# Cross attention on one core: which engine makes the weight low parts, and the order of copies and exponentials in the first steps

## The reference

```
h = layernorm(x) * gamma + beta
Q = h @ Wq;  K = context @ Wk;  V = context @ Wv          # per head 64 wide
attn = softmax(Q @ K^T, axis=-1) * 64 ** -0.5
out = x + (attn @ V).reshape(256, 1024) @ Wo + bo
```

## Time and profile before

| | us |
|---|---|
| median of 3 runs | 364.79 (364.53 to 364.80) |
| the profiled execution: its own time | 364.5 |
| its span, from the first to the last instruction of the trace | 362.6 |
| TensorE matmul busy | 353.0 (97%) |
| ScalarE busy | 252.1 (70%) |
| VectorE busy | 242.9 (67%) |
| GpSimd busy | 164.5 (45%) |

### The profile page before, as it was taken

One profiled execution on the slowest core, in us unless ns is written; L12 is line 12 of the kernel. 1 busy time (PEld: TensorE's weight loads), 2 busy tenths in 40 slices (PEclk: granted clock), 3 DMA queues, 4 the chain that ended last, 5 costly groups with the idle time before them and its releaser, 6 DMA issues.

```text
span 362.6 us, 8915 instructions
## 1 busy us (share of the span) xinstructions
PE 353.0 (97%) x3116; PEld 305.8 (84%) x3116; DVE 242.9 (67%) x534; ACT 252.1 (70%) x762; POOL 164.5 (45%) x321
## 2 busy tenths in 40 slices
PE   5999999999999999999999999999999999999986
PEld 5779888888888888988888988888988888988865
DVE  5887566866568666686667675686565866566654
ACT  4898876766677766777766776766677766677762
POOL 5677884335444262444532464323744325344321
PEclk9999999999999999999999999999999999999999
DMA  6930010200002000020000100020000000000000
GB/s 191 272 118 3 1 52 2 82 0 3 2 0 82 0 0 0 0 80 0 1 0 29 51 0 0 0 78 1 0 0 0 29 2 0 2 2 31 3 0 31
DMA packets 10743, 10.39 MB, mean 29 GB/s; under 512 B 960, under 2 KB 10176, under 8 KB 10720
## 3 DMA queue, kind: packets, MB, share of 16 engines
q1 hardware_dynamic: 10192, 9.64, 8.6%
q10 hardware_dynamic: 416, 0.33, 0.3%
q0 software_dynamic: 112, 0.13, 0.2%
HBM read 8.00 MB, written 2.10 MB: 28 GB/s over the span
## 4 chain that ended last, share of the span: by engine, by line
PE 92%; ACT 3%; DVE 3%; DMA 1%; issue 0%; POOL 0%; DVEq 0%
PE mix_ps L710 16%; PE st_ps L805 15%; PE st_ps L688 13%; PE o_ps L777 12%; PE w_ps L752 12%; PE w_ps L730 12%; PE w_ps L823 10%; ACT prob L405 2%; DMA x_in<-in_x_dram 1%; PE w_ps L671 1%; PE w_ps L663 1%; ACT qk_hi L415 0%; DVE w_lo L480 0%; DVE neg_max L563 0%; DVE qk_lo L576 0%
## 5 line engine op out<-in xcount | busy, mean ns | idle before, releaser
L316 POOL TENSOR_SCALAR prob<-prob,inv 128x256 f32<-128x256 f32 x256 | 120.1, 485 | 158.0 <-DVE inv L570 157.6
L405 ACT ACTIVATE prob<-st_ps,neg_max 128x256 f32<-128x256 f32 x256 | 118.0, 473 | 27.0 <-DVE neg_max L563 27.0
L563 DVE TENSOR_REDUCE neg_max<-st_ps 128x2 f32<-128x512 f32 x128 | 82.5, 683 | 35.2 <-PE st_ps L688 34.9
L458 ACT ACTIVATE prob_t<-st_ps 128x512 f32<-128x512 f32 x64 | 38.4, 600 | 44.2 <-PE st_ps L805 44.2
L638 DVE COPY prob_t<-st_ps 128x512 f32<-128x512 f32 x64 | 44.1, 691 | 28.6 <-PE st_ps L805 25.2
L710 PE MATMUL mix_ps<-prob_t,v_sb 128*64 128x256 f32 x504 | 61.5, 385 | 0.1
L805 PE MATMUL st_ps<-ident,prob 128*128 128x128 f32 x512 | 61.1, 272 | 0.0
L805 PEld LDWEIGHTS st_ps<-ident,prob 128*128 128x128 f32 x512 | 56.7, 141 | 0.1
L576 DVE TENSOR_TENSOR qk_lo<-w_ps,qk_hi 128x512 fp32r<-128x512 f32 x62 | 42.8, 690 | 20.6 <-ACT qk_hi L415 20.6
L405 ACT ACTIVATION_READ_ACCUMULATOR prob<-st_ps,neg_max 128x1 f32 x256 | 52.7, 206 | 0.0
L710 PEld LDWEIGHTS mix_ps<-prob_t,v_sb 128*64 128x64 f32 x504 | 33.4, 136 | 17.9 <-issue 0.3
(11 more groups left out here) (121 smaller groups left out, 589.1 us busy)
## 6 DMA issues: line engine op xcount, KB each, us to landing
x_in<-in_x_dram SPq DMA_DIRECT2D x8, 256.0 KB, 3.1
out_dram<-y_sb SPq DMA_DIRECT2D x7, 256.0 KB, 2.2
c_in<-in_ctx_dram SPq DMA_DIRECT2D x7, 192.0 KB, 2.9
w_raw<-in_L_xattn_Wq_dram SPq DMA_DIRECT2D x8, 128.0 KB, 3.3
w_raw<-in_L_xattn_Wo_dram SPq DMA_DIRECT2D x4, 256.0 KB, 3.5
w_raw<-in_L_xattn_Wk_dram SPq DMA_DIRECT2D x4, 128.0 KB, 4.0
w_raw<-in_L_xattn_Wk_dram SPq DMA_DIRECT2D x8, 64.0 KB, 3.6
w_raw<-in_L_xattn_Wv_dram SPq DMA_DIRECT2D x2, 256.0 KB, 3.5
```

The lines of the kernel that those rows point to most:

```text
L316: last = nc.gpsimd.tensor_scalar(prob[:, e, r, :], prob[:, e, r, :], inv[:, e, r:r + 1], SCALE, ALU.mult, ALU.mult)
L405: last = nc.scalar.activation(prob[:, e, r, :], st_ps[e][:, r * ROWS:(r + 1) * ROWS], ACT.Exp, bias=neg_max[:, e, r:r + 1], accum_out=sums ...
L458: nc.scalar.activation(prob_t[:, e, :, :].rearrange("p a b -> p (a b)"), st_ps[e][:, :], ACT.Copy)\
L563: nc.vector.tensor_reduce(neg_max[:, e, :], st_ps[e][:, :].rearrange("p (r j) -> p r j", r=RT), AX, ALU.max, negate=True).then_inc(max_rea ...
```

## The change

Three low parts (4, 5, 8) go from VectorE to GpSimd and one (14) from GpSimd to VectorE. In step 0, VectorE scales the heads 1 and 3 itself (`scale`), with its own semaphore. On ScalarE, in step 0 the exponential of head 3 comes before `keys_hi(0)`, the high parts 11 to 13 go behind the copies, `context_hi(1)` moves from the head of step 1 to ahead of them; in step 1 the high part of 14 takes the place of 15, and 15 goes behind `keys_hi(1)`, ahead of 16. VectorE makes low part 9 between `maximum(1)` and `maximum(2)` of step 0, and does the statistics of sequence 1 and low part 13 behind the copies of step 0. GpSimd issues the load of `bo` later. TensorE's order is unchanged.

```diff
-    LO_VECTOR = (0, 4, 5, 8, 9, 13, 16)
-    LO_POOL = (1, 2, 3, 6, 7, 10, 11, 12, 14, 15, 17, 18, 19, 20, 21, 22, 23)
+    LO_VECTOR = (0, 9, 13, 14, 16)
+    LO_POOL = (1, 2, 3, 4, 5, 6, 7, 8, 10, 11, 12, 15, 17, 18, 19, 20, 21, 22, 23)
@@ GpSimd
-            for n in (1, 2, 3, 6, 7):
+            for n in (1, 2, 3, 4, 5, 6, 7, 8):
                 weight_lo(n)
-            pool.dma_start(bo_b[:, :], b_o.partition_broadcast(P)).then_inc(bo_in, 16)
@@ step
-                if u == 1:
-                    weight_lo(14)
...
-                    for e in range(HEADS):
+                    for e in (0, 2) if u == 0 else range(HEADS):
...
                         if e == 1 and u in (1, 2):
                             weight_lo({1: 15, 2: 21}[u])
+                if u == 0:
+                    pool.dma_start(bo_b[:, :], b_o.partition_broadcast(P)).then_inc(bo_in, 16)
@@ ScalarE
-                b = of_seq(u, SPLIT_C, 1)
+                b = of_seq(u, SPLIT_C, 2)
@@
-                if u == 1:
-                    weight_hi(14)
                 probabilities(0)
                 probabilities(1)
                 if u in (1, 2):
-                    weight_hi({1: 15, 2: 21}[u])
+                    weight_hi({1: 14, 2: 21}[u])
@@
                 probabilities(2)
+                if u == 0:
+                    probabilities(3)
                 keys_hi(0)
...
-                probabilities(3)
+                if u != 0:
+                    probabilities(3)
                 keys_hi(1)
...
                 if u == 0:
                     values_out(0, w0_ps)
-                    weight_hi(10)
-                    weight_hi(11)
                     values_out(1, w1_ps)
+                if u == 1:
+                    weight_hi(15)
                 if u == 1:
                     weight_hi(16)
@@
                         if u == 0 and e == 0:
-                            weight_hi(12)
-                            weight_hi(13)
+                            weight_hi(10)
+                if u == 0:
+                    act.wait_ge(c_turned, 2)
+                    context_hi(1, context_bank(1))
+                    for n in (11, 12, 13):
+                        weight_hi(n)
@@ VectorE
+                def scale(e):
+                    dve.wait_ge(inv_ready, e + 1)
+                    for r in range(RT):
+                        last = nc.vector.tensor_scalar(prob[:, e, r, :], prob[:, e, r, :],
+                                                       inv[:, e, r:r + 1], SCALE,
+                                                       ALU.mult, ALU.mult)
+                    last.then_inc(scaled_vector, 1)
                 maximum(0)
                 maximum(1)
+                if u == 0:
+                    weight_lo(9)
@@
                 inverse(1)
                 if u == 0:
-                    weight_lo(8)
-                    weight_lo(9)
+                    scale(1)
+                if u == 1:
+                    weight_lo(14)
@@
                 inverse(2)
-                if u == -1:
-                    weight_lo(4)
+                if u == 0:
+                    inverse(3)
+                    scale(3)
                 keys_lo(0)
-                if u == -1:
-                    weight_lo(5)
-                inverse(3)
+                if u != 0:
+                    inverse(3)
@@
                 keys_lo(1)
-                if u == 0:
-                    statistics(1, turns)
@@ behind and within the copies of heads 1 and 3
-                        if u == 0 and e == 1:
-                            weight_lo(13)
+                if u == 0:
+                    statistics(1, turns)
+                    weight_lo(13)
@@ TensorE, turn
-                    pe.wait_ge(scaled, HEADS * u + e + 1 + turns(32))
+                    if u == 0:
+                        pe.wait_ge((scaled, scaled_vector)[e % 2], e // 2 + 1)
+                    else:
+                        pe.wait_ge(scaled, HEADS * u + e - 1 + turns(32))
```

More of the change, by code:

```diff
@@ L154, in cross_attention_block @@
         scaled = sem("scaled")
+        scaled_vector = sem("scaled_vector")
         turned = sem("turned")
```

## The result

| | before | changed |
|---|---|---|
| median, us | 364.80 (6 runs, 364.53 to 364.82) | 367.81 (6 runs, 367.67 to 369.37) |
| profiled execution, its span | 364.5, 362.6 | 367.8, 365.9 |

By the medians the kernel is slower by 3.0 us (a ratio of 1.0083); 367.5 was forecast. The ratio over all runs is 1.0096 (95% interval 1.0076 to 1.0115). It is higher because two of the six runs, 369.13 and 369.37, are a group of their own, with a mean granted clock of 0.995 and 0.994 where the other four have 1.000.

What follows compares the result with a forecast made beforehand. TensorE, 92% of the chain, was taken as the bound. Head 3 of `turn(1)` starting 2.7 us later gave 364.5 + 2.7 = 367.2, as a median 367.5; this case alone 366.6 to 368.1, whole range 366.2 to 369.2.

Steps and rivals of the forecast that it cites:

- The mechanism: Step 1: GpSimd's in-order queue holds heads 2 and 3 behind low part 15, which waits for late high part 15; +2.7 us.
- second half of `scores(0)`: Step 0, TensorE: starts about 0.2 sooner than 13.54 without low part 5 ahead of `keys_lo(1)`.
- step 1's exponentials start: ScalarE, step 1: at 24.1 instead of 23.66, 0.4 later; bounds 0 or 0.9.
- high part 15 starts, is ready: ScalarE, step 1, behind `keys_hi(1)`: starts at 29.75, takes 0.65, ready at 30.4; before, it was made at 25.47.
- the port: Step 1: VectorE's low part 16 waits for GpSimd's low part 15, and head 2 for 16; 0.5, bounds 0 and 0.6.
- head 3's transposes: TensorE, `turn(1)`: head 3 starts at 34.1 instead of about 31.4, +2.7 us.
- TensorE's lead behind `scores(1)`: TensorE some 1.2 to 1.5 ahead after `scores(1)`, through three removed waits; used up in the wait at `turn(1)`.
- wait ahead of `output(0)`: TensorE, step 1: new wait of about 1.4; `mix_lo` comes at about 28.5, TensorE at 27.1.
- point 1: Start: low part 5 off VectorE ahead of `keys_lo(1)` starts second half of `scores(0)` about 0.2 sooner, at most 0.3.
- Rival A: TensorE's clock falls during its new idle time in step 1, costing 1.7 more: +4.4, 369.2; chance 0.31.
- Rivals B and C: B: faster, TensorE keeps its lead, 363.5, chance 0.03. C: no change, 364.8 to 365.2, chance 0.04.
- the late exponentials: Step 1, next late once low part 15 is out of the way: heads 2 and 3 scaled 0.4 to 0.5 behind before.

Runs made afterwards that it cites:

- e3: Kernel before, with only high part 15 moved behind `keys_hi(1)` of step 1 on ScalarE: 367.14 us, ratio 1.0073.
- e2: Changed kernel, with GpSimd's low part 15 moved behind head 3 of step 1, high part 15 still late: 365.25 us, ratio 1.0014.
- e6: Kernel of e2, with GpSimd holding low part 4 until VectorE has made both `h_lo`: 364.70 us, ratio 1.0000 to the kernel before.
- e7: Kernel of e6, with VectorE's low part 13 moved behind the second maximum of step 1: 363.96 us, ratio 0.9982 to the kernel before.
- e9: Kernel of e1, with VectorE's low part 16 held until GpSimd has scaled heads 2 and 3 of step 1: 365.65 us, ratio 1.0031.
- e8: Changed kernel, with VectorE's low part 16 held until GpSimd has scaled heads 2 and 3 of step 1: 367.36 us, ratio 1.0082.
- e4: Kernel before, with only low parts 4 and 5 moved from VectorE to GpSimd: 365.12 us, ratio 1.0014.
- e5: Kernel of e2, with low parts 4 and 5 back on VectorE: 364.80 us, ratio 1.0003 to the kernel before.
- e1: Changed kernel, with high part 15 moved back directly behind that of 14 on ScalarE: 366.35 us, ratio 1.0044 to the kernel before.

## Why the prediction was right, and where it was off

**The mechanism was the forecast's.** GpSimd's in-order queue held heads 2 and 3 behind a piece that ScalarE now makes last. e3 shows that this move is enough, e2 that its loss is taken back by the queue's order alone.

**The terms.**

| term | forecast | measured |
|---|---|---|
| second half of `scores(0)` | 13.3 | 14.18 |
| step 1's exponentials start | 24.1 | 24.73 |
| high part 15 starts, is ready | 29.75, 30.4 | 30.29, 31.0 |
| low part 15 | 1.28 | 1.27 |
| the port | 0.5 | 0.4 (2.29 less 1.90) |
| head 3's transposes | 34.1 | 34.66 |
| `values(0)` no longer waits | 0.44 gained | gone (17.10, next pass 17.80) |
| `scores(1)` starts | 21.0 | 21.68 |
| second half of `scores(1)` | no wait | at 22.49, no wait |
| TensorE's lead behind `scores(1)` | 1.2 to 1.5 | 0.80 (`mix(0)` at 23.29, 24.09 before) |
| wait ahead of `output(0)` | 1.4 | 0.91 |
| `scores(2)` starts | 36.2 | 36.84 |

From the exponentials on, every start is late by 0.54 to 0.64, and the lead of TensorE is short by 0.4 to 0.7. That is the one step that failed: under "what the change saves", point 1 took 0.2 as gained at the start. It was a loss, the second half of `scores(0)` being 0.64 later than before and 0.88 later than forecast. I had checked whether low parts 4 and 5 are ready in time on GpSimd, and not what they take from VectorE while they run. The rows that show it in the changed kernel:

```profile
9.80 0.43 DVE L532 TENSOR_TENSOR h_lo<-h_full,h_hi 128x256 fp32r<-128x256 f32 x1
10.15 0.95 DVE L535 TENSOR_TENSOR h_lo<-h_full,h_hi 128x256 fp32r<-128x256 f32 x1
```

GpSimd's low part 4 started at 9.88. Not all of the later start is the edit. TensorE worked at the lower clock for longer in this profile: the record of its granted clock in the trace begins at full speed 9.6 us into the span, and at 7.1 in the profile before (ahead of its first entry the views print 1.00), and four transposes of x took 1.12 at 7.26 where they took 0.66. This varies from run to run. The eleven profiles let the two be told apart by the start of the first half of `scores(0)`:

| full clock from | low part 4 not on GpSimd, or held (e6, e7) | low part 4 on GpSimd at once |
|---|---|---|
| 6.8 to 7.1 us | 12.26 (before), 12.25 (e6) | 12.78 (e9) |
| 7.8 to 8.0 us | none | 13.54 (e8), 13.57 (e4) |
| 8.9 to 9.7 us | 12.54 (e3), 12.52 (e5), 12.52 (e7) | 13.08 (changed), 13.06 (e1), 13.07 (e2) |

The late clock goes with 0.26 to 0.30 in either kind, low part 4 on GpSimd with 0.52 to 0.56 in the first and the last row; in the middle row it is more, since both `h_lo` are stretched there (0.90 and 0.94 in e8). By medians e5 and e6 put the price at 0.45 to 0.55. What point 1 did claim is true by itself: in e6, with the two low parts off VectorE and held back, the second half of `scores(0)` starts at 13.35, 0.19 sooner than before. The same exclusion was priced about rightly 20 us later, and was not looked for here.

That the median is off by only 0.3, less than the price of this step, is in part luck: with the start set right (e6) the exponentials of step 1 start at 23.90, 0.2 sooner than the 24.1 of the forecast, so two errors went against each other. TensorE's shorter lead mattered little, since it was to be used up in the wait at `turn(1)` and was. (The weights are 24 pieces, 0 to 23, and not 25; nothing here hangs on the count.)

**The port.** VectorE's low part 16 in the changed kernel:

```profile
31.54 1.35 DVE L486 TENSOR_TENSOR w_lo<-w_raw,w_hi 128x512 fp32r<-128x512 f32 x1
```

It took 1.35 and the multiplications 2.29 when both wanted to run, 0.69 and 1.85 when one was made to wait (e8). It started at 31.54, while low part 15 was running until 32.34, and ended at 32.89; the first multiplication, started at 32.31, took 0.92 and then ended at 33.23. The Trainium skill, "SBUF — State Buffer", section "SBUF: two separate sides", has the pair of ports locked by one of the two engines for a whole instruction while the other stands. These runs agree: VectorE lost 0.66, less than the 0.80 for which GpSimd's low part still ran, and GpSimd lost 0.44, less than the 0.69 of low part 16.

**Rival A happened too, in some of the runs.** In e8's profiled execution the clock fell. Its busy time by stretch (TensorE, weight load, VectorE, ScalarE, GpSimd, then granted clock):

```profile
32.00:34.00 2.00, 0.24 (x2) 0.24 (x3) 0.69 (x1) 0.44 (x1) 2.00 (x4) 1.00 0.00 0
34.00:36.00 2.00, 1.75 (x10) 1.37 (x9) 1.26 (x2) 1.55 (x5) 1.17 (x3) 0.78 0.00 0
36.00:38.00 2.00, 2.00 (x8) 1.53 (x6) 0.12 (x1) 0.70 (x2) 2.00 (x4) 0.50 0.03 8
38.00:40.00 2.00, 2.00 (x26) 1.58 (x24) 0.58 (x1) 1.18 (x3) 0.23 (x1) 0.87 0.00 0
```

From 36 to 38 it is 0.50, that is 1.2 instead of 2.4 GHz, though TensorE had begun to work again at 33.76; by the shares of the stretches beside it, it fell at about 35.1 and was back at about 38.5. The three passes of `values(2)` take 1.60 there:

```profile
35.08 1.60 PE L845 MATMUL w_ps<-w_hi,c_t 128*128 128x512 f32 x3
```

against 0.94 in the changed kernel's profile. The fall followed the 1.8 us wait at `turn(1)`, and costs 1.3 to 2.0: 369.13 and 369.37 against 367.7 to 367.8 in the changed kernel, 368.60 and 369.30 against 367.3 in e8, 368.51 against 367.1 in e3. It was seen in 5 of the 17 runs of the three kernels that have a wait of 1.7 to 2.2 us at `turn(1)` (changed, e3, e8), and in none of the 66 runs of the seven that have not. That the wait makes it is argued from this count; no run was made to show it alone. The forecast's 1.7 for it lies within the 1.3 to 2.0. Its chance of 0.31 was for the whole result and cannot be compared with 5 runs in 17: in none of the three kernels does the median show the fall.

**Rivals B and C** fell with the wait of 2.2 us. The forecast said that the late exponentials come next once low part 15 is out of the way, and gave them 0.4 to 0.5, through the scaling of heads 2 and 3. They do come next, and e7 took back 0.74 by them, but by another way: in e2 and e6 TensorE has no wait at `turn(1)`, and the exponentials hold it at `output(0)`, through `mix_lo`.

## What to carry to other kernels

When an instruction moves on one engine, look at every queue in which something waits for it, and at what stands behind that waiter: in an in-order queue these are held too, though they need nothing from it. An instruction moved to GpSimd must be checked twice, for when its result is wanted and for what VectorE does meanwhile. In 5 of 17 runs here the clock fell after a wait of TensorE of about 2 us and added 1.3 to 2.0 us; a median of few runs hides that, the list of runs shows it.

## What the runs showed of the hardware

TensorE's clock can fall for a stretch after a wait of about 2 us, and not in every run of the same kernel: 2 of 6, 1 of 6 and 2 of 5 here. In e8 it fell after TensorE had already resumed work (at about 35.1; the work at 33.76) and was low until about 38.5, so the price does not end with the wait.

A VectorE copy from SBUF to SBUF (`h_hi`) is held beside GpSimd as well, and not only the subtractions with two inputs. In eight profiles it started between 8.88 (e8) and 9.34 (e5), while the same low part was running on GpSimd, which ended at 9.60 to 9.62 where no other followed at once (changed, e3, e5, e7). It took from 0.88 (e8) down to 0.42 (e5), and ended at 9.75 to 9.77 in all eight. Read so, a long duration in such a row is for the most part time spent waiting for the other engine; no run was made to test this reading for a copy.
